# Expert loop of a routed FFN: token gather in front of the scatters, slot tables inside layer 1, last expert's sum on VectorE

## What is computed

```
xf = cond(x).reshape(N, D)                       # N = 4096, D = 512
probs = softmax(xf @ gate_w.T)                   # 8 experts
scores_sel = _xmoe_route(probs)                  # threshold 0.9, per expert the best 512 tokens, else 0
h = gelu(einsum('nd,efd->enf', xf, w1))          # F = 512
y_e = einsum('enf,edf->end', h, w2)
y = einsum('ne,end->nd', scores_sel, y_e)
return x + y
```

## Time and profile before

| | |
|---|---|
| time, median of 3 runs | 296.15 us (295.68 to 299.74) |
| the profiled execution, its own time | 298.54 us |
| its span, first to last instruction | 296.7 us |
| TensorE matmul busy | 246.0 us (83%), 1328 matmuls |
| VectorE busy | 205.8 us (69%) |
| ScalarE busy | 154.1 us (52%) |
| GpSimd busy | 135.5 us (46%), 100 instructions |
| mean granted clock of TensorE | 0.914 |

### The profile page before, as it was taken

One profiled execution on the slowest core, in us unless ns is written; L12 is line 12 of the kernel. 1 busy time (PEld: TensorE's weight loads), 2 busy tenths in 40 slices (PEclk: granted clock), 3 DMA queues, 4 the chain that ended last, 5 costly groups with the idle time before them and its releaser, 6 DMA issues.

```text
span 296.7 us, 3852 instructions
## 1 busy us (share of the span) xinstructions
PE 246.0 (83%) x1328; PEld 185.0 (62%) x1328; DVE 205.8 (69%) x501; ACT 154.1 (52%) x285; POOL 135.5 (46%) x100
## 2 busy tenths in 40 slices
PE   0866686845699999699899979979997999999960
PEld 0544342111458888588688858858886888888740
DVE  5399978988456996686799588676967966952100
ACT  5421116754037765765766567475556657744310
POOL 0000000004876268647847755771776388580260
PEclk9996959566579999999999999997999999999995
DMA  6999989801383049627916962890497269164082
GB/s 243 424 423 417 509 309 300 299 3 38 106 313 115 0 54 334 178 38 179 327 28 84 342 143 35 228 296 9 57 322 188 36 145 241 12 77 58 0 106 35
DMA packets 12418, 52.33 MB, mean 176 GB/s; under 512 B 2656, under 2 KB 2912, under 8 KB 9184
## 3 DMA queue, kind: packets, MB, share of 16 engines
q1 hardware_dynamic: 4208, 35.31, 32.2%
q0 software_dynamic: 8192, 16.80, 29.1%
HBM read 43.58 MB, written 17.96 MB: 207 GB/s over the span
## 4 chain that ended last, share of the span: by engine, by line
PE 35%; DMA 19%; POOL 16%; DVE 12%; issue 9%; ACT 5%; POOLq 1%; SPq 0%; ACTq 0%; DVEq 0%
DMA xg<-in_x,gath 17%; PE bank L740 9%; PE bank L742 9%; PE bank L741 9%; POOL out L269 8%; POOL xg L254 8%; PE bank L720 3%; PE bank L802 2%; ACT region L395 2%; DVE xg L581 2%; DMA region<-in_xt 2%; DVE region L629 2%; ACT ysb L338 1%; PE bank L781 1%; DVE csum L587 1%
## 5 line engine op out<-in xcount | busy, mean ns | idle before, releaser
L269 POOL DMA_INDIRECT out<-ysb,scat x32 | 62.4, 1949 | 64.5 <-ACT ysb L338 60.3
L254 POOL DMA_INDIRECT xg<-in_x,gath x32 | 39.9, 1247 | 79.2 <-DVE gath L517 69.8
L461 DVE SCALAR_TENSOR_TENSOR w1rot<-w1raw,rot,w1rot 128x512 f32<-128x512 f32 x84 | 63.1, 751 | 5.1 <-issue 1.8
L740 PE MATMUL bank<-w2h,hh 128*128 128x512 f32 x128 | 51.9, 406 | 0.0
L741 PE MATMUL bank<-w2l,hh 128*128 128x512 f32 x128 | 50.6, 396 | 0.0
L742 PE MATMUL bank<-w2h,hl 128*128 128x512 f32 x128 | 50.5, 395 | 0.0
L740 PE MATMUL bank<-xh,w1h 128*128 128x512 f32 x128 | 49.9, 390 | 0.3 <-DVE xl L484 0.3
L741 PE MATMUL bank<-xl,w1h 128*128 128x512 f32 x128 | 49.8, 389 | 0.0
L742 PE MATMUL bank<-xh,w1l 128*128 128x512 f32 x128 | 49.8, 389 | 0.0
L490 DVE TENSOR_TENSOR hl<-hf,hh 128x512 fp32r<-128x512 f32 x32 | 22.1, 689 | 36.2 <-ACT hh L329 36.2
L338 ACT ACTIVATE ysb<-bank,score 128x512 f32<-128x512 f32 x32 | 22.1, 689 | 37.3 <-PE bank L742 37.3
(11 more groups left out here) (126 smaller groups left out, 325.5 us busy)
## 6 DMA issues: line engine op xcount, KB each, us to landing
region<-in_xt SPq DMA_DIRECT2D x8, 1024.0 KB, 9.0
w1raw<-in_w SPq DMA_DIRECT2D x8, 1024.0 KB
w2raw<-in_w SPq DMA_DIRECT2D x8, 1024.0 KB
xg<-in_x,gath POOLq DMA_INDIRECT x32
score<-probs_scratch,pidx POOLq DMA_INDIRECT x32
out<-ysb,scat POOLq DMA_INDIRECT x32, 4.9
ch<-in_ch SPq DMA_DIRECT2D x1, 368.5 KB, 7.8
cf<-in_cf SPq DMA_DIRECT2D x1, 149.0 KB, 2.4
```

The costliest lines, as they stand in the source:

```text
L254: pool.indirect_dma_start(xg[:, s, :], None, x_d, bass.IndirectOffsetOnAxis(gath[:, e, s:s + 1], 0)).then_inc(xg_in[s], 16)
L269: pool.indirect_dma_start(out_d, bass.IndirectOffsetOnAxis(scat[:, e, s:s + 1], 0), ysb[:, s, :], None, compute_op=ALU.add).then_inc(added ...
L461: ins = nc.vector.scalar_tensor_tensor(dst, w1raw[:, e % 2, i, :], rot[:, j, i:i + 1], dst, ALU.mult, ALU.add)
L740: nc.tensor.matmul(dst, ah, bh, start=first, stop=False)
```

## The change

On GpSimd `gather_x(e + 2)` stands in front of the four scatters of expert e. Its slot table is made earlier: TensorE's `slot_rows(e + 2)` stands between `layer1(e, 1)` and `layer1(e, 2)`, VectorE's `slots_after(e + 2)` in front of `h_low(e, 0)` and `slot_tables(e + 2)` between `h_low(e, 1)` and `h_low(e, 2)`. In the prologue `count_before(1, 2, E)` takes the place of two `keep_clock` matmuls in front of the last tile's transposes, and ScalarE copies its result just before the last tile. For the last expert, GpSimd gathers the rows of `out` at the expert's slots into `xg` once all scatters of expert 6 have landed; VectorE (`y_sum`) multiplies the product by the score and adds the gathered row, and the four scatters write without an addition. ScalarE has no `y_out` for it.

```diff
@@ -37,6 +37,7 @@
 C4 = D // P
 F4 = F // P
 S4 = CAP // P
+LAST = E - 1
 TG = 512
 NG = N // TG
 TPG = TG // P
@@ -262,12 +263,21 @@
                                             bass.IndirectOffsetOnAxis(pidx[:, e, s:s + 1], 0)).then_inc(score_in[e % 2], 16)
 
             def scatter(e, s):
-                if e >= 1 and s == 0:
+                if 1 <= e < LAST and s == 0:
                     for k in range(S4):
                         pool.wait_ge(added[k], 16 * e)
                 pool.wait_ge(y_ev, S4 * e + s + 1)
-                pool.indirect_dma_start(out_d, bass.IndirectOffsetOnAxis(scat[:, e, s:s + 1], 0),
-                                        ysb[:, s, :], None, compute_op=ALU.add).then_inc(added[s], 16)
+                pool.indirect_dma_start(out_d, bass.IndirectOffsetOnAxis(scat[:, e, s:s + 1], 0), ysb[:, s, :], None,
+                                        compute_op=ALU.add if e < LAST else ALU.bypass).then_inc(added[s], 16)
+
+            def gather_sums():
+
+                pool.wait_ge(xt_mm, C4 * E)
+                for k in range(S4):
+                    pool.wait_ge(added[k], 16 * LAST)
+                for s in range(S4):
+                    pool.indirect_dma_start(xg[:, s, :], None, out_d,
+                                            bass.IndirectOffsetOnAxis(scat[:, LAST, s:s + 1], 0)).then_inc(xg_in[s], 16)
 
             pool.wait_ge(probs_out, 16)
             gather_x(0)
@@ -276,12 +286,12 @@
             gather_scores(1)
             pool.wait_ge(out_base, 32)
             for e in range(E):
-                scatter(e, 0)
-                scatter(e, 1)
+                if e == LAST:
+                    gather_sums()
                 if e + 2 < E:
                     gather_x(e + 2)
-                scatter(e, 2)
-                scatter(e, 3)
+                for s in range(S4):
+                    scatter(e, s)
                 if e + 2 < E:
                     gather_scores(e + 2)
 
@@ -407,9 +417,9 @@
             w2_high(0)
 
             nc.scalar.activation(warm[:, :], cfv("ident")[:, 0:1], ACT.Gelu)
-            x_high0(0)
-            rows_out(1, 2, E)
-            for s in range(1, S4):
+            for s in range(S4):
+                if s == S4 - 1:
+                    rows_out(1, 2, E)
                 x_high0(s)
             w1_first(1, 0)
             for e in range(E):
@@ -430,18 +440,16 @@
                     x_high(e + 1, 1)
                     w1_first(e + 1, 3)
                     w1_high(e + 1, 2)
-                y_out(e, 0)
-                if more:
+                    y_out(e, 0)
                     x_high(e + 1, 2)
                     x_high(e + 1, 3)
                     w1_high(e + 1, 3)
-                y_out(e, 1)
-                if more:
+                    y_out(e, 1)
                     w2_high(e + 1)
-                y_out(e, 2)
-                if e + 2 < E:
-                    w1_first(e + 2, 0)
-                y_out(e, 3)
+                    y_out(e, 2)
+                    if e + 2 < E:
+                        w1_first(e + 2, 0)
+                    y_out(e, 3)
 
         @block.vector
         def _(dve):
@@ -670,12 +678,14 @@
                     w2_low(e)
                 if more:
                     rotate_w1(e + 1, 0)
+                if later:
+                    slots_after(e + 2)
                 h_low(e, 0)
                 if more:
                     rotate_w1(e + 1, 1)
                 h_low(e, 1)
                 if later:
-                    slots_after(e + 2)
+                    slot_tables(e + 2)
                 h_low(e, 2)
                 if more:
                     rotate_w1(e + 1, 2)
@@ -687,10 +697,22 @@
                     rotate_w1(e + 1, 3)
                     x_low(e + 1, 2)
                     x_low(e + 1, 3)
-                if later:
-                    slot_tables(e + 2)
                 if more:
                     w1_low(e + 1, 0, C4)
+
+            def y_sum(s):
+
+                n = S4 * LAST + s
+                dve.wait_ge(y_mm, n + 1)
+                if s == 0:
+                    dve.wait_ge(score_in[LAST % 2], 16 * S4 * (LAST // 2 + 1))
+                dve.wait_ge(added[s], 16 * LAST)
+                dve.wait_ge(xg_in[s], 16 * (E + 1))
+                nc.vector.scalar_tensor_tensor(ysb[:, s, :], ybank[n % 2][:, :], score[:, LAST % 2, s:s + 1], xg[:, s, :],
+                                               ALU.mult, ALU.add).then_inc(y_ev, 1)
+
+            for s in range(S4):
+                y_sum(s)
 
         @block.tensor
         def _(pe):
@@ -728,7 +750,7 @@
                         last = nc.tensor.transpose(x0bank(s)[:, j, :], xg[:, s, j * P:(j + 1) * P], ident)
                     last.then_inc(xt_mm, 1)
                     if s == S4 - 2:
-                        keep_clock(2)
+                        count_before(1, 2, E)
 
             def keep_clock(n):
 
@@ -864,18 +886,19 @@
             slot_rows(1)
             keep_clock(3)
             transpose_x0()
-            count_before(1, 2, E)
             keep_clock(7)
             for e in range(E):
-                for f in range(F4):
-                    layer1(e, f)
+                layer1(e, 0)
+                layer1(e, 1)
+                if e + 2 < E:
+                    slot_rows(e + 2)
+                layer1(e, 2)
+                layer1(e, 3)
                 if e + 1 < E:
                     transpose_x(e + 1, (0, 1))
                 layer2(e, 0)
                 if e + 1 < E:
                     transpose_x(e + 1, (2, 3))
-                if e + 2 < E:
-                    slot_rows(e + 2)
                 for s in range(1, S4):
                     layer2(e, s)
```

## The result

| | before | after |
|---|---|---|
| time, median | 296.67 us (295.68 to 299.74, 4 runs) | 284.75 us (282.36 to 285.51, 4 runs) |
| ratio | | 0.958, 95% interval 0.953 to 0.964 |
| the profiled execution, its own time | 298.54 us | 284.87 us |
| its span | 296.7 us | 283.1 us |

The account below looks back on a forecast made before the run. TensorE was taken as the bound, waiting in the expert loop for late token gathers. From the median: 296.15 - 9.8 (waiting) + 0.3 (tables) - 1.0 (start) - 1.5 (end) = 284.15, said as 284.2 us; range 281 to 288.5.

Parts of the forecast that it names:

- the forecast case: Whole kernel: the change works as predicted, 284.2 us; chance 0.82.
- The other sum: Whole kernel, from the profiled execution: 298.54 - 11.35 + 0.3 - 1.0 - 1.5 = 285.0 us.
- Where the gather goes (1): Expert loop, GpSimd: gather before the scatters starts 7.0 us earlier, 11 us of cover, all 9.8 us of waiting go.
- My worst case for this step: Gather in the loop: four instructions of 2.95 us, then 9.6 us, land at 198.5; loss 0.4 us per expert, 2.4 in all.
- The tables (1, 3): Expert loop: slot table at 181.83 would be too late, so made in layer 1; cost 0 to 0.6 us, taken 0.3.
- the fourth h_low: VectorE in the expert loop: the next to be late from the moved tables; TensorE already waited 0.7 us in 2 places.
- Scatters behind the gather (2): Expert loop: scatter 0 starts at 185.0 instead of 179.60, with 17.5 us open for a 4.9 us landing; cost nothing.
- Start (4): Prologue: layer 1 loses 1.3 us of counting and waiting, 0.3 go back at half clock; bounds 0 and 1.4, taken 1.0.
- The sign that the clock would be 1.00 from layer 1 on: TensorE's granted clock: 1.00 from layer 1 on was listed among the signs that the forecast is right.
- End (5): Last expert: scatter without addition saves 0.6 us of issue and 0.9 of landing, about 1.5; bounds 0 and 2.5.
- The clock: TensorE in the loop: 1.57 us of half clock may belong to the profiled execution alone; with it 282.6 us.
- Rival B: VectorE is held by gathers beside x_low and w1_low, late by 1.4 us per expert, 8.4 in all: 292.6 us; chance 0.04.

Follow-up runs that it names:

- loop-only kernel: Kernel before with the gather in front of the four scatters and slot rows and tables inside layer 1, prologue and last expert unchanged: 285.95 us, ratio 0.960.
- prologue-only: Kernel before with only the counts of experts 2 to 7 in place of two prologue fillers: 297.8 us, ratio 0.994.
- last-expert-only: Kernel before with only the last expert's gather of the sums, addition on VectorE and scatter without addition: 295.91 us, ratio 0.986.
- the kernel with the late w2_low: Changed kernel with VectorE's w2_low of expert 0 behind the prologue's four x_low instead of in front: 282.45 us, ratio 0.950.
- the one with three fillers: Changed kernel with w2_low of expert 0 behind the x_low and three filler matmuls instead of seven before layer 1: 281.99 us, ratio 0.948.

## Why the prediction was right, point by point

**The sum.** 284.2 us was said, 284.75 measured; the forecast case came true and its mechanism is shown by the loop-only kernel. The other sum, against the profiled execution before, said 285.0, and the profiled execution after took 284.87. That both came within 0.6 us is in part luck: measured beside each other once more the kernels were 14.5 us apart (297.75 and 283.28), not 12. The terms against the profiled executions:

| term | said | measured |
|---|---|---|
| lost in six periods | 11.35 with the clock, 0.3 given back | 11.07, 0.33 given back for the slot rows that moved from the first period into layer 1 |
| start | 1.0 | 0.95: layer 1 starts 1.69 earlier, 0.74 go back at half clock |
| end | 1.5 | 1.95 less 0.04 |

**Where the gather goes (1).** Right in the result, wrong in the cover. I wrote that the last issue ends at 184.7, 5.8 us after 178.9, and that the tokens lie there 2.5 us later, with 11 us to spare. Measured from the transposes, issue ends at 13.21 and not at 10.5, because two of the four instructions take 2.4 us beside w1_low and w2_low, and the last lands 9.3 us after its start and not 3.5, with the weights issued at 12.4, before it ends. In the one round with a single weight load (from 216.28) it was 7.4. The cover is 3.9 us. My worst case for this step (four instructions of 2.95 and 9.6 us) had the right ingredients; the value I took did not.

**The tables (1, 3).** The sentence that a table done at 181.83 would be too late is false. With the gather first and the tables late the gather starts 3.6 us later than in the changed kernel, and nobody waits, with 0.5 us to spare. The moved tables buy 3.4 us of cover. Their price from the start of layer 1 to expert 7's transposes is 0.4 us (11.32 + 143.71 in the loop-only kernel against 10.97 + 143.65 with late tables), mostly in expert 0's layer 1, where I took 0.3. The path I named for it, the fourth h_low, is not shown: TensorE's waits for h_low did grow from 0.7 us in 2 places to 2.0 in 8, but to 1.9 in 8 also with the tables left late, so it is not the tables that made them.

**Scatters behind the gather (2).** Nothing was paid, as said. ScalarE's y_out waits only for TensorE in the list of waits.

**Start (4).** The count and the wait went as said, and layer 1 began at 84.16, 0.4 us before the 84.55 worked out from 1.3. But its first products ran at half clock to about 85.5, and layer 1 took 12.06 us (96.22 less 84.16) against 10.99. Of that, 0.33 come with the slot rows, since the loop-only kernel takes 11.32 at full clock; the other 0.74 are the half clock, where 0.3 was said. The sign that the clock would be 1.00 from layer 1 on was not met. That the sum of this part came out (0.95 for 1.0) is luck: 1.69 stood for 1.3 and 0.74 for 0.3. In the changed kernel measured once more the clock rose earlier and only 0.26 us went back; counted from the first gather instruction, its transposes of expert 1 came 1.16 us earlier than in the kernel before, and 0.69 in the first execution. The term depends on the execution.

**End (5).** The issue went from 1.54 to 0.95 us, as said. The landing, from the instruction's end, went from 3.36 to 1.75 us, where the bound taken from a gather was 2.5. So 2.2 us came at the landing and 1.95 in the span; all executions with and without the addition differ there by 1.9 to 2.2 us. The gather of the sums ended its issue at 265.15 and was used from 266.85 on, without a wait.

**The clock.** I left its 1.57 us out of the median. The loop-only kernel gained 12.9 us against its own before, more than 9.8 (just so at the end of its interval, 9.95), and the profiles of the prologue-only and last-expert-only kernels show transposes of 1.94 us, that is half clock, behind standstills of 2.9 and 3.0 us. So half clock occurs in other executions of that loop too, in all three that were profiled with its full waits, and leaving it out of the median was not justified by them; how often it occurs and what it costs in the median is not measured.

**Rival B and the port.** The rotations on VectorE stayed at 741 to 756 ns in the changed kernel with 144.5 us of GpSimd beside them:

```profile
L469 DVE SCALAR_TENSOR_TENSOR w1rot<-w1raw,rot,w1rot x84: 741/752/756, 83.0 to 245.5; 128x512 f32<-128x512 f32 x84
```

B is out. Of the rule in the Trainium skill (SBUF — State Buffer, "Who interferes with whom") the runs show one half only: a VectorE subtraction with two SBUF inputs holds GpSimd's instruction (2.95 us, and 0.94 with the subtraction moved away). The other half, VectorE held by GpSimd, shows in none of these rows: w1_low at 175.62 began while the gather instruction from 175.02 to 175.97 was under way, and took its usual 2.28 us.

**What I did not see.** The kernel before could have been mended by one swap of two VectorE steps, for 10.4 of the 14.5 us that the changed kernel gains beside it. The row that pointed to it was before me: scatter 1 took 2.6 us in its rounds against 1.6 for scatter 0, and I did not ask what it ran beside. I also took the gather's lateness as a matter of its issue alone, while the moment of the weights' issue is tied to the same VectorE order.

## What to carry over

When an indirect DMA on GpSimd is late, look first at which of its neighbours in the queue lasts longer than its kind (here 2.6 against 1.6 us) and what VectorE does at that moment: putting one large two-input subtraction in front of the tables (it began 0.2 to 1.0 us earlier, and the weights were issued up to 0.6 us later) was worth nearly as much as reordering the whole queue. When such a swap helps, look at all that it moves before naming the cause. A cover should be worked out with the slowest duration its new neighbours can give and with the transfers that will be in flight, not with the quiet-queue figure. And while a loop waits for a transfer, time won ahead of it may not arrive at the end: measure such edits on the kernel in which the wait is already gone, and count positions from the last common event, since prologues differ by more than the gain.

## What the runs showed of the hardware

- A scatter of 128 rows of 2 KB without addition was issued in 0.95 us and landed 2.7 us after its start; with addition it took 1.54 and 4.9 us on quiet queues, and a median of 7.2 from its start to its landing over the changed kernel, where it runs beside the weights.
- In the loop the granted clock fell to half behind standstills of TensorE of 1.9 and 2.0 us (once each, in the prologue-only kernel and the kernel before) and behind each of 2.6 to 5.1 us, but not behind others of 1.96, 2.3 and 2.4. In the prologue it rose in 85 to 86 in the kernel before and the changed kernel, in 83 to 84 in the changed kernel measured once more, in 81 to 82 in the kernel with the late w2_low and near 80 in the one with three fillers.
- A VectorE subtraction of 128x2048 with two SBUF inputs took 2.27 to 2.29 us (once 2.33) with or without GpSimd beside it. A gather instruction that began beside it ended 0.8 to 0.9 us after it, early or late as it began, and so took between 1.36 us (begun at 12.72 beside one that ended at 13.19, behind the transposes at 96.84 of the kernel before) and 2.95 us, instead of 0.94.
- From the last landing to the end of the span 4.1 to 4.4 us passed, with and without the addition.
